# Fifteen multiplications of the second attention, on VectorE in the place of GpSimd

## The reference, cut to what matters

```python
a = einsum('nhtd,nhsd->nhts', q, k) / sqrt(64)      # n = 2, t = s = 1024, h = 16
a = softmax(where(mask, -inf, a), axis=-1)
y = einsum('nhts,nhsd->nthd', a, v)
return y.reshape(n, t, 1024) @ w_o
```

## Time and profile before

| | us |
|---|---|
| runs, median of 3 (lowest, highest) | 805.47 (804.61, 806.94) |
| the profiled execution | 800.03 |
| its span, first to last instruction | 798.2 |
| mean granted TensorE clock, share of full speed | 0.959 |
| VectorE busy, 704 instructions | 532.1 (67%) |
| ScalarE busy, 495 instructions | 450.9 (56%) |
| GpSimd busy, 367 instructions | 466.8 (58%) |

### The profile page before, as it was taken

One profiled execution on the slowest core, in us unless ns is written; L12 is line 12 of the kernel. 1 busy time (PEld: TensorE's weight loads), 2 busy tenths in 40 slices (PEclk: granted clock), 3 DMA queues, 4 the chain that ended last, 5 costly groups with the idle time before them and its releaser, 6 DMA issues.

```text
span 798.2 us, 21288 instructions
## 1 busy us (share of the span) xinstructions
PE 725.3 (91%) x9393; PEld 429.3 (54%) x9406; DVE 532.1 (67%) x704; ACT 450.9 (56%) x495; POOL 466.8 (58%) x367
## 2 busy tenths in 40 slices
PE   3667888888888899998999999999999999999997
PEld 1533454445335444554565565555776655676764
DVE  7699967889778765777675575556536556753037
ACT  2424769986575689555636655665444665546312
POOL 6815567600850300499968777877655986667840
PEclk9855989999899999999999999999999999999999
DMA  8000000000000000000001111001101101111110
GB/s 271 2 1 2 3 2 3 2 3 2 2 2 2 2 3 2 2 2 5 27 4 26 29 30 29 10 22 28 30 2 28 29 3 29 29 29 30 28 29 26
DMA packets 13223, 16.18 MB, mean 20 GB/s; under 512 B 3052, under 2 KB 10572, under 8 KB 13132
## 3 DMA queue, kind: packets, MB, share of 16 engines
q1 hardware_dynamic: 12556, 14.50, 6.3%
q10 hardware_dynamic: 576, 0.33, 0.2%
HBM read 13.26 MB, written 1.17 MB: 18 GB/s over the span
## 4 chain that ended last, share of the span: by engine, by line
PE 70%; DVE 17%; POOL 5%; ACT 5%; issue 3%; DMA 0%; ACTq 0%; POOLq 0%; DVEq 0%
PE ps L1228 19%; PE ps L1177 16%; DVE big L1054 9%; PE ps L1156 6%; PE ps L1398 5%; PE ps L1207 5%; PE ps L1435 3%; ACT Pr L811 3%; PE ps L1403 2%; PE ps L1352 2%; PE ps L1238 2%; POOL acts L672 1%; DVE moments L1004 1%; PE ps L1346 1%; PE ps L1318 1%
## 5 line engine op out<-in xcount | busy, mean ns | idle before, releaser
L1081 DVE TENSOR_REDUCE mxb<-ps 128x8 f32<-128x1024 f32 x144 | 173.3, 1222 | 90.4 <-PE ps L1228 61.3
L672 POOL TENSOR_TENSOR V0s<-V0s,Pr 128x1024 f32<-128x1024 f32 x77 | 182.1, 2365 | 62.7 <-ACT Pr L840 31.0
L1054 DVE TENSOR_REDUCE big<-ps 128x8 f32<-128x1024 f32 x144 | 168.9, 1218 | 27.9 <-PE ps L1207 16.6
L811 ACT ACTIVATE Pr<-ps,exp_scale 128x1024 f32<-128x1024 f32 x144 | 154.8, 1114 | 44.4 <-PE ps L1207 31.5
L840 ACT ACTIVATE Pr<-ps,exp_scale 128x1024 f32<-128x1024 f32 x112 | 119.5, 1114 | 90.3 <-PE ps L1228 72.9
L1228 PE MATMUL ps<-big 64*128 64x128 f16 (+2 forms) x2560 | 168.9, 259 | 0.7 <-DVE mxb L1081 0.4
L1207 PE MATMUL ps<-big 32*128 32x128 f16 (+2 forms) x1280 | 102.4, 279 | 35.7 <-DVE big L1054 22.2
L1228 PEld LDWEIGHTS ps<-big 64*128 64x128 f16 x2560 | 92.8, 94 | 71.6 <-issue 17.0
L1177 PE MATMUL ps<-Pr,V1s 128*64 128x128 f32 (+2 forms) x960 | 111.3, 371 | 0.0
L1207 PEld LDWEIGHTS ps<-big 32*128 32x128 f16 x1280 | 40.4, 95 | 108.5 <-DVE big L1054 53.1
L587 POOL TENSOR_TENSOR stats<-moments 128x8 f32<-128x8 f32 x9 | 1.9, 210 | 163.7 <-DVE moments L1004 163.7
(11 more groups left out here) (242 smaller groups left out, 921.7 us busy)
## 6 DMA issues: line engine op xcount, KB each, us to landing
rec_b<-scratch_dram SPq DMA_DIRECT2D x30, 256.0 KB, 3.9
X<-in_x_dram SPq DMA_DIRECT2D x2, 256.0 KB, 3.8
big<-in_pick_rows_dram SPq DMA_DIRECT2D x2, 256.0 KB, 3.0
X<-in_x_dram SPq DMA_DIRECT2D x1, 512.0 KB, 5.4
rec_b<-in_w_q_dram SPq DMA_DIRECT2D x1, 512.0 KB, 5.8
XT<-in_w_k_dram SPq DMA_DIRECT2D x1, 512.0 KB, 6.6
XT<-in_w_v_dram SPq DMA_DIRECT2D x1, 512.0 KB, 7.3
wo_s<-in_w_o_dram SPq DMA_DIRECT2D x1, 512.0 KB, 8.1
```

Source lines behind the costliest of these rows:

```text
L672: g.tensor_tensor(dst, dst, src, ALU.add).then_inc(summed, 1)
L811: a.activation(group_buf[e_no % GROUP_BUFS], by_head(slot), ACT.Exp, scale=exp_scale[0][:, 0:1]).then_inc(slot_act, 1)
L1054: v.tensor_reduce(maxima_of(mall[:, r, 2 * u:2 * u + 2], i), block_view(by_head(slot), i), AX.X, ALU.max, negate=True).then_inc(slot_dve, 1)
L1081: v.tensor_reduce(maxima_of(mxb[:, r], arg), block_view(by_head(slot), arg), AX.X, ALU.max, negate=True).then_inc(slot_dve, 1)
```

## The change

norm_pair moves from GpSimd's program into VectorE's, with the same waits, operands and semaphore, and is called at the same step of PLAN; in VectorE's program that is behind the row maxima that come earlier in PLAN and ahead of those that come later. The last call moves to VectorE's first place after PLAN, ahead of the reciprocal of the last pair (L1105). Nothing else differs.

```diff
@@ GpSimd's program @@
-            def norm_pair(p):
-                pool.wait_ge(acc1_saved, p + 1)
-                pool.wait_ge(rec_in, 32 * (p + 1))
-                if p == 0:
-                    pool.wait_ge(slot_filled, filled("gkq", G - 1, None))
-                if p >= NP:
-                    pool.wait_ge(slot_filled, filled("wo", 0, (0, NP, WO_PARTS - 1)))
-                g.tensor_tensor(YT[:, p % NP], y_raw[p % 2], rec_b[:], ALU.mult).then_inc(normed, 1)
...
                 if kind == "exp":
-                    if arg == NORM_AT and key >= 2:
-                        norm_pair(key - 2)
...
-            norm_pair(LAST - 1)
@@ VectorE's program @@
+            def norm_pair(p):
+                dve.wait_ge(acc1_saved, p + 1)
+                dve.wait_ge(rec_in, 32 * (p + 1))
+                if p == 0:
+                    dve.wait_ge(slot_filled, filled("gkq", G - 1, None))
+                if p >= NP:
+                    dve.wait_ge(slot_filled, filled("wo", 0, (0, NP, WO_PARTS - 1)))
+                v.tensor_tensor(YT[:, p % NP], y_raw[p % 2], rec_b[:], ALU.mult).then_inc(normed, 1)
...
+                if kind == "exp" and arg == NORM_AT and key >= 2:
+                    norm_pair(key - 2)
                 done = key - 1 if kind == "exp" and arg == REC_AT else -1
...
+            norm_pair(LAST - 1)
             dve.wait_ge(ln_read, len(NORM_NO))
             dve.wait_ge(last_turned, 1)
```

## The result

| | before | changed |
|---|---|---|
| runs, median (lowest, highest) | 805.47 (803.19, 806.94), 5 runs | 814.71 (809.90, 815.92), 5 runs |
| ratio, 95% interval | | 1.0124 (1.0095 to 1.0152) |
| span of the profiled execution | 798.2 | 808.1 |
| VectorE busy (instructions) | 532.1 (704) | 554.5 (719) |
| GpSimd busy (instructions) | 466.8 (367) | 433.6 (352) |

A forecast was written before the change was run, and what follows sets the result against it. TensorE was taken to pace the stage, with GpSimd having next to nothing to give. Delays of 2.4 + 2.8 + 0.4 + 0.3 + 0.8 + 0.3 = 7.0 us made the profiled 800.03 into 807.0; plus 5.4 gave 812.5, range 806.5 to 818.0.

The forecast's parts named there:

- The price of one: One multiplication on VectorE: rest of GpSimd's running instruction plus 1.2 us; 1.2 with GpSimd idle, 3.6 at worst.
- The wait for rec_b: New wait on VectorE with row maxima queued behind it; in pair 3, 6.1 us from reciprocal to data.
- Pair 3: Multiplication starts at 475.1 and ends at 476.3, next row maxima 2.9 us late; TensorE loses 2.4 us.
- Pair 4: rec_b is there, but a GpSimd addition is running; row maxima 3.3 us late, cost 2.8 us.
- Pairs 1, 8, 12: Next row maxima 3.0, 0.5 and 2.1 us late; costs 0.4, 0.3 and 0.8 us.
- Pair 9: Multiplication fits into idle time of VectorE; cost 0, or about 1 us if that cover were missing.
- Pair 7: First sequence's output projection: an earlier product offset by later row maxima freeing the projection's slot; even, 0.
- Pair 14: At the end, the last pair's reciprocal stands behind the multiplication in VectorE's queue; cost 0.3 us.
- the first (1.2 us everywhere): Rival: VectorE pays 1.2 us everywhere and waits for rec_b remain; about 4.4 us, 809.9; chance 0.24.
- The second rival: Dearer: landings 1 us later, an addition ahead of pair 12's multiplication; 12 us, 817.5; chance 0.15.
- Covered: Rival: delays are real, but TensorE's slack or VectorE's catching up hides them; 0 to 2 us, 806.5; chance 0.17.
- faster: Rival: relieved GpSimd paces the chunks, so ScalarE and TensorE run ahead; gain under 1 us plus projection, 804.6; chance 0.06.

The follow-up runs named there:

- again: The changed kernel run once more, unaltered, for a second profile; 814.02 us, ratio 1.0132.
- one-in: The changed kernel with each multiplication replaced by a VectorE maximum over y_raw, one input in SBUF, same place and waits; 808.81 us, ratio 1.0057.
- only4: The kernel before, with the multiplication of pair 4 alone moved to VectorE; 808.89 us, ratio 1.0052.
- early-rec: The changed kernel with the reciprocals of pairs 3 and 14 made earlier in the order; 811.17 us, ratio 1.0078.
- wait: The kernel before, multiplications on GpSimd, with VectorE also standing at the fifteen places until y_raw and rec_b are there; 806.46 us, ratio 1.0030.

## Why the prediction held, point by point

The forecast was 812.5 us in a range of 806.5 to 818.0; measured were 814.7. The sum was 7.0 us in the stage; the two profiles have 8.2 and 10.5. The mechanism was as forecast at the large places; one term, pair 4, was too small by the clock, and in the first profile the errors of the small terms cancel by luck (pair 9 0.5 more than said, pairs 7 and 14 0.5 less together).

- **TensorE paces the stage, GpSimd has nothing to give.** Shown by the run without multiplications: no more than 0.02 us gained until the projection, then 0.75 there. The wait of 0.2 us on GpSimd stayed, as said. The prediction's "for GpSimd once, for 0.2 us" passed over the 0.6 us before L1435, which the list puts down to no engine.
- **The price of one.** It was read from two instructions of 1.71 and 2.71 us and from GpSimd's stretched ones. The changed kernel has 1.2 us where GpSimd rests and 2.3, 2.6, 1.9 and 3.1 us in pairs 0, 1, 2 and 4 (1.4 in pair 13), each time ending 1.1 us behind the end of the running addition; the additions beside them take up to 3.2. The counter-run with one input stays at 1.22. In this kernel it is the rest of the running GpSimd instruction plus 1.1 to 1.2 us, for an instruction with both inputs in SBUF. The rule of the Trainium skill, "GPSIMD Engine Reference", § 8 Key points, on two SBUF inputs, agrees with these numbers. The narrower list in the Trainium skill, "Advanced Engine Details and Errata", § VectorE Performance Modes, does not cover it, and the measurement decides.
- **The wait for rec_b.** 6.0 us from reciprocal to landing in most pairs (5.8 to 7.5), as read; VectorE idle for 2.52 us in pair 3, against 2.6 forecast.
- **Pair 3:** forecast 2.4, measured 2.29 in one profile and 4.0 in the other, where the clock fell and rec_b came 0.2 us later.
- **Pair 4:** forecast 2.8, measured 4.08 and 4.03. The stall was right, 2.22 us of idle time; the mis-sized term is the clock behind it, which I had at 1.00 throughout. The prediction named a falling clock among what would make it wrong, but gave it no term. At full clock (the run with the earlier reciprocal) pair 4 cost 2.67.
- **Pairs 1, 8, 12:** forecast 0.4, 0.3, 0.8; measured 0.36, 0.25, 0.91.
- **Pair 9:** forecast 0, measured 0.52. VectorE's own cover was there, but I had not followed what the multiplication does to GpSimd: it held the running series of additions up once (3.21 us in the place of 2.36),

```profile
644.70 3.21 POOL L662 TENSOR_TENSOR V0s<-V0s,Pr 128x1024 f32<-128x1024 f32 x1 [0.17 <-POOL V0s L662]
```

  and the reduction of pair 10's sums (L1239), which TensorE comes to right behind the last addition, waited 0.4 us for it.
- **Pair 7:** forecast even, measured -0.20 in one profile and +0.5 in the other, where rec_b landed 0.7 us later; the run without multiplications shows that 0.75 us were to be had there, which the late row maxima gave back.
- **Pair 14:** forecast 0.3, measured 0: rec_b landed at 777.50, and the last reciprocal waited for TensorE as before.

Of the rivals, the first (1.2 us everywhere) is what the run with one input shows, but for its clock; the changed kernel is not it. The second rival, later landings, happened in the second profile in small: 0.2 us in pair 3 and 0.7 in pair 7, each passed on in full. No rival had the clock. "Covered" and "faster" are out. What stays open: what makes the clock fall behind one stall and not behind another that is as long or longer (it fell behind 1.85 us and stayed up behind 2.24).

## What to carry to other kernels

Before moving an instruction to an engine with idle time, ask what is queued behind it there and how soon its results are wanted: 68% busy in the stretch says little, while the 0.7 to 0.8 us between the end of a row maximum and the reuse of its slot, as the prediction reads them at pairs 3 and 4, and the time at which the data land say most of it. The same fifteen instructions cost 9 us at one set of places and nothing once six of them stood later. A wait and an instruction that are each covered need not be covered together (pair 12), and when a matmul engine that was never idle starts to stall for 2 us, count its clock as well.

## What was not expected of the hardware

- A stall of TensorE of 1.9 to 2.2 us was followed by windows of 2 us with a granted clock down to 0.50 to 0.59 in five of the seven such stalls seen here (pair 3 in "again" and "one-in", pair 4 in "changed", "again" and "only4", and not in pair 3 of "changed" nor pair 4 of "early-rec"), worth some 1.4 to 1.7 us where a profile with and one without it can be compared. The shorter stalls, of 1.2 us (wait) and 1.4 us (pair 3 of early-rec), were not.
- The profiles of kernels that do the same up to 376 us differed there by up to 6 us, with granted clocks of 0.93 and 1.00 in the same stretch; a comparison of spans would have put that down to the change.
- The store of 8 KB in front of the broadcast took 1.3 us at most pairs, but 2.1 to 2.7 at pair 5 and 2.9 to 3.4 at pair 14 in every profile but one (1.3, where pair 14's reciprocal came earlier), and 3.6 at pair 3 of that run. Long stores and a packet of 16 KB with instructions within 2 us of the issue go together in all 180 cases.
